# Who adds the second experts' sums: GpSimd's two passes or VectorE's, and the order of a round around them

## What is computed

```python
# end of the second layer's ffn: its two experts per token are summed, then normalized with a gain
fused = sum((topk_vals[:, :, i:i + 1] * outs[i] for i in range(TOP_K)))
return _layer_norm(residual + fused, ln_gamma, ln_beta)
...
# third layer, attention block (mLSTM), 4 heads of 64
D = jnp.exp(log_D - max_log_D)
C = qk * D
normalizer = jnp.maximum(jnp.abs(C.sum(-1, keepdims=True)), jnp.exp(-max_log_D))
h = jnp.einsum('bnst,bntd->bnsd', C / (normalizer + EPS_BACKEND), vh)
hn = (h - mean) * jax.lax.rsqrt(var + NORM_EPS) * outnorm_weight
...
# third layer, feed-forward block, with x_prev the token before
xr = mu_r * x + (1.0 - mu_r) * x_prev
xk = mu_k * x + (1.0 - mu_k) * x_prev
r = jax.nn.sigmoid(jnp.einsum('btc,dc->btd', xr, W_r))
k_act = jnp.square(jax.nn.relu(jnp.einsum('btc,dc->btd', xk, W_k)))
out = r * jnp.einsum('btc,dc->btd', k_act, W_v)
```

## Time and profile before

| | us |
|---|---|
| median of 3 runs | 1398.53 |
| lowest and highest run | 1395.99, 1401.62 |
| the profiled execution | 1400.19 |
| its span | 1398.1 |
| TensorE busy in it | 1258.8 (90%) |
| VectorE busy | 852.8 (61%) |
| ScalarE busy | 474.4 (34%) |
| GpSimd busy | 463.3 (33%) |

### The profile page before, as it was taken

How to read it: one execution, slowest core, us unless ns; L and a number is a source line. 1 busy time by engine, 2 the same in 40 slices (tenths; PEclk the granted TensorE clock), 3 DMA queues, 4 the chain that set the end, 5 groups by cost and what they waited for, 6 DMA issues and landing times. The chain is left out here.

```text
span 1398.1 us, 31670 instructions
## 1 busy us (share of the span) xinstructions
PE 1258.8 (90%) x9966; PEld 1008.9 (72%) x9966; DVE 852.8 (61%) x2809; ACT 474.4 (34%) x1119; POOL 463.3 (33%) x435
## 2 busy tenths in 40 slices
PE   5899799997899998899999888897899998899995
PEld 4677589995566665789887666686566665799995
DVE  5788544445577876444575476755567776465563
ACT  3555211112556554011111244453556654111110
POOL 1145612223134334423122256533134343222231
PEclk9999899999999999999999998999999999999998
DMA  9101234422111401464655100000001011646523
GB/s 312 66 17 36 93 103 139 136 65 80 34 36 40 164 33 51 140 205 149 198 174 168 28 8 1 1 1 24 8 17 48 32 40 53 207 100 150 145 46 87
DMA packets 87556, 120.07 MB, mean 86 GB/s; under 512 B 11248, under 2 KB 64752, under 8 KB 87152
## 3 DMA queue, kind: packets, MB, share of 16 engines
q1 hardware_dynamic: 48656, 55.20, 12.9%
q10 hardware_dynamic: 25632, 34.85, 7.6%
q0 software_dynamic: 13152, 28.54, 7.2%
HBM read 82.53 MB, written 38.13 MB: 86 GB/s over the span
## 5 line engine op out<-in xcount | busy, mean ns | idle before, releaser
L1349 PEld LDWEIGHTS bank<-f_xT,f_up 128*128 128x128 f32 x2144 | 253.6, 192 | 13.3 <-issue 6.3
L1349 PE MATMUL bank<-f_xT,f_up 128*128 128x128 f32 x2144 | 258.5, 276 | 2.4 <-DVE f_xT L1225 2.1
L415 DVE TENSOR_REDUCE mha_nmax<-bank 128x2 f32<-128x512 f32 x256 | 170.0, 686 | 117.2 <-PE bank L558 93.5
L1358 PE MATMUL bank<-f_down,f_hT 128*128 128x256 f32 x832 | 199.5, 382 | 4.4 <-DVE f_hT L1266 2.3
L308 ACT ACTIVATE l_took<-bank 128x512 f32<-128x512 f32 x256 | 139.0, 598 | 129.8 <-PE bank L566 129.8
L558 PE MATMUL bank<-l_took,mha_q 32*128 32x256 f32 x1024 | 146.3, 402 | 34.5 <-DVE mha_nmax L415 22.1
L1358 PEld LDWEIGHTS bank<-f_down,f_hT 128*128 128x128 f32 x832 | 149.4, 190 | 24.8 <-DVE f_hT L1266 4.6
L1114 POOL DMA_INDIRECT yout<-f_y,f_to x66 | 81.1, 1229 | 244.9 <-DVE f_y L1302 107.0
L558 PEld LDWEIGHTS bank<-l_took,mha_q 32*128 32x128 f32 x1024 | 90.1, 186 | 74.5 <-DVE mha_nmax L415 45.0
L566 PE MATMUL bank<-l_took 32*128 32x256 f32 x1024 | 142.8, 400 | 0.7 <-ACT l_took L308 0.7
L1165 ACT ACTIVATE f_hT<-bank,f_b 128x128 f32<-128x128 f32 x148 | 46.4, 364 | 276.0 <-PE bank L1349 276.0
(11 more groups left out here) (293 smaller groups left out, 2284.9 us busy)
## 6 DMA issues: line engine op xcount, KB each, us to landing
l_took<-rows SPq DMA_DIRECT2D x91, 132.0 KB
f_up<-in_W ACTq DMA_DIRECT2D x23, 512.0 KB, 4.8
f_down<-in_W ACTq DMA_DIRECT2D x18, 512.0 KB, 5.4
l_took<-rows SPq DMA_DIRECT2D x21, 264.0 KB
f_up<-in_W SPq DMA_DIRECT2D x9, 512.0 KB, 7.3
ring<-yout SPq DMA_DIRECT2D x8, 512.0 KB, 3.9
mha_ctxT<-in_ctxT SPq DMA_DIRECT2D x16, 256.0 KB, 2.9
f_down<-in_W SPq DMA_DIRECT2D x6, 512.0 KB, 7.5
```

What stands on the lines that cost most here:

```text
L415: vector.tensor_reduce(nmax[:, p, :, at], ps_s[n % 2][:, :].rearrange("p (k s) -> p k s", s=S), AX.X, ALU.min).then_inc(max_ready, 1)
L1349: ins = pe.matmul(into, up[q][i][:, c, m * P:(m + 1) * P], xT[:, c, :], start=c == 0, stop=c == DC - 1)
L1358: ins = pe.matmul(ps_y[:, 0:D], hT[:, m, :], down[q][:, m, :], start=m == 0, stop=m == HC - 1)
```

## The change

Six things, all in l2:

- GpSimd's z_add is gone, and VectorE's z_normalize. VectorE does z_centre and z_in for all batches: in rounds 0 to 4 z_centre stands where z_normalize stood, and z_in at the end of the round. GpSimd's z_root_of comes ahead of normalize instead of behind it.
- VectorE's f_normalize comes ahead of gate_rows.
- mean_and_var and z_mean_and_var come ahead of the weights of heads 2 and 3; they stood behind them, the latter behind the first mix.
- ScalarE's squares come ahead of squared_relu.
- On TensorE, the values of heads 0 and 1 come ahead of turn_f; a fill of 1 stands between the second spread and turn_z in rounds 1 to 7 (it stood in round 7 alone); round 0's fill of 1 becomes 2; turn_m comes ahead of turn_x.
- z_scaled and z_gained, two semaphores, are gone.

```diff
@@ gpsimd
-            def z_add(b):
-                pool.wait_ge(z_scaled, b + 1 - RING)
-                z_ = fused[:, b % RING, :, :]
-                pool.tensor_tensor(z_, z_, gamma[:, :].unsqueeze(1).to_broadcast([P, TPB, D]), ALU.mult).then_inc(z_gained, 1)
-                pool.wait_ge(z_gained, b + 1 - RING)
-                x = X[:, pair(b), :]
-                pool.tensor_tensor(x, x, z_, ALU.add).then_inc(z_added, 1)
...
+                if w_ + 3 < B:
+                    z_root_of(w_ + 3)
                 if w_ + 2 < B:
                     normalize(w_ + 2)
-                if w_ + 3 < B:
-                    z_root_of(w_ + 3)
-                    z_add(w_ + 3)
@@ scalar
-                if w_ >= LAG:
-                    squared_relu(w_ - LAG)
                 if now:
                     squares(w_)
                 if w_ >= LAG:
+                    squared_relu(w_ - LAG)
                     receptance(w_ - LAG)
@@ vector
-            def z_normalize(b):
...
@@ vector, the round
-                if more:
-                    gate_rows(w_ + 1)
                 if w_ >= LAG:
                     f_normalize(w_ - LAG)
                 if more:
+                    gate_rows(w_ + 1)
                     gates_in(w_ + 1)
+                if w_ + 2 < B:
+                    mean_and_var(w_ + 2)
+                if w_ + 3 < B:
+                    z_mean_and_var(w_ + 3)
                 if now:
                     weigh(w_, 2)
                     weigh(w_, 3)
-                if w_ + 2 < B:
-                    mean_and_var(w_ + 2)
                 if w_ >= LAG:
                     mix(w_ - LAG, 1, k_mixed)
-                if w_ + 3 < B:
-                    z_mean_and_var(w_ + 3)
...
                 if w_ + 3 < B:
-                    z_normalize(w_ + 3)
+                    z_centre(w_ + 3)
...
                 if w_ >= LAG:
                     outputs(w_ - LAG)
+                if w_ + 3 < B:
+                    z_in(w_ + 3)
@@ tensor
-                if w_ == B - 1:
+                if now and w_:
                     fill(w_, 1)
                 if more:
                     turn_z(w_ + 1)
                 if now:
                     qk(w_, 1)
+                    values(w_, 0)
+                    values(w_, 1)
...
-                if now:
-                    values(w_, 0)
-                    values(w_, 1)
                 if w_ == 0:
-                    fill(w_, 1)
+                    fill(w_, 2)
...
+                if more:
+                    turn_m(w_ + 1)
                 if w_ + 2 < B:
                     turn_x(w_ + 2)
-                if more:
-                    turn_m(w_ + 1)
```

More of the change, by code:

```diff
@@ L1869, in l2 @@
         fused_in, gamma_in = [sem(f"fused{r}_in") for r in range(RING)], sem("gamma_in")
-        z_ready, z_root, z_scaled, z_gained, z_added = sem("z_ready"), sem("z_root"), sem("z_scaled"), sem("z_gained"), sem("z_added")
+        z_ready, z_root, z_added = sem("z_ready"), sem("z_root"), sem("z_added")
         w, mu = sb("w", [P, 3, DC, D]), sb("mu", [P, 2, DC])
@@ L2114, in z_mean_and_var @@
                 moments_of(z_moments, z_stats, z_var, z_ready, b, fused[:, b % RING, :, :])
-            def z_normalize(b):
-                vector.wait_ge(z_root, b + 1)
-                for i in range(TPB):
-                    z_ = fused[:, b % RING, i, :]
-                    ins = vector.tensor_scalar(z_, z_, z_moments[:, b, i, 0:1], z_rstd[:, b, i:i + 1], ALU.subtract, ALU.mult)
-                ins.then_inc(z_scaled, 1)
             def z_centre(b):
@@ L2125, in z_centre @@
                 for i in range(TPB):
-                    z_ = fused[:, b, i, :]
+                    z_ = fused[:, b % RING, i, :]
                     ins = vector.scalar_tensor_tensor(out=z_, in0=z_, scalar=z_moments[:, b, i, 0:1], in1=gamma[:, :],
@@ L2134, in z_in @@
                     x = X[:, TPB * b + i, :]
-                    ins = vector.scalar_tensor_tensor(out=x, in0=fused[:, b, i, :], scalar=z_rstd[:, b, i:i + 1], in1=x,
+                    ins = vector.scalar_tensor_tensor(out=x, in0=fused[:, b % RING, i, :], scalar=z_rstd[:, b, i:i + 1], in1=x,
                                                       op0=ALU.mult, op1=ALU.add)
```

## The result

| | before | after |
|---|---|---|
| median, us | 1398.28 (6 runs) | 1392.73 (6 runs) |
| lowest and highest | 1395.99, 1401.62 | 1389.21, 1394.83 |
| span of the profiled execution | 1398.1 | 1391.8 |
| third layer, its begin to K8 | 195.7 | 190.3 |

What follows compares the result with a forecast made beforehand. The prediction took VectorE's line of work to bound the kernel. Its terms, -2.1 - 7.9 - 1.2 + 2.5 + 1.3 - 2.0 = -9.4 us, taken from the median 1398.53, gave 1389 us, range 1383 to 1399.

Steps and rivals of the forecast that it cites:

- Steps 1 and 3: Round from project_k: z_centre before gains hidden (0.88 us); TensorE, reaching turn_z after the gates' rows, holds the line by 1.
- The rival of small steps: Handovers in rounds 0 to 6 cost half a microsecond more each: +5 to 6 us, about 1394.5, chance 0.15.
- Step 2, the late relu: Squares before the relu delay TensorE's project_v, costing 0.7 us in rounds 1 to 6 with nothing to hide it.
- Step 4, z_in: Before f_mean_and_var, held beside GpSimd's passes over h: 0.2 to 0.6 us at worst, within slack, counted 0.
- Step 5 and the port: Copy of z to next project_k: 5.2 us. Rival: GpSimd's xn passes block the mixes, +6, 1395, chance 0.17.
- the rule that spoke against the forecast: Skill's rule: VectorE instructions with two SBUF inputs and GpSimd's SBUF reads fully block, holding mixes for a whole xn pass.
- Round 0: Round 0 and the way to round 1's project_k: VectorE earlier, partly held by turn_m and spread, -2.1 us.
- K1 to K4: Three rounds between project_k starts of rounds 1 and 4: 66.7 us becomes 3 x 19.6 = 58.8, -7.9.
- K4 to K5: Project_k of round 4 to that of round 5: 20.7 us becomes 19.5, the difference waiting for fT, -1.2.
- K5 to K6, K6 to K7: Project_k of rounds 5 to 7, no z batch left to save: 17.0 becomes 19.5 (+2.5), 16.2 becomes 17.5 (+1.3).
- K7 to the end: Tail from round 7's project_k: VectorE's 2.33 us wait for squares behind the relu goes, -2.0.
- a rival that decides for all rounds or none: TensorE's granted clock dips while its work is in the line: +3 us per round, 1404 to 1407, chance 0.11.

Runs made afterwards that it cites:

- the second measurement: The changed kernel run once more, unchanged, in a later job: 1397.01 us, ratio 0.9986.
- orders_only: The changed kernel with the z batch handed back to z_normalize and GpSimd's z_add, all new orders kept: 1396.07 us, ratio 0.9982.
- z_only: The kernel before with VectorE's z_centre and z_in for all batches, GpSimd's two passes gone, old orders kept: 1386.71 us, ratio 0.9890.
- fill_waits: The changed kernel with a dummy matmul in TensorE's waits before the last heads' values and before project_k: 1392.24 us, ratio 0.9944.
- turnf_first: The changed kernel with turn_f ahead of the first two heads' values again, in all rounds: 1394.61 us, ratio 0.9952.
- z_stats_fill: z_stats with a fill of one before the last heads' values and one before project_k, rounds 1 to 7: 1390.51 us, ratio 0.9945.
- z_stats: z_only with the statistics of X and the z batch ahead of the weights of heads 2 and 3: 1389.81 us, run again 1390.02.

## Why the prediction was right, and where its size was off

A gain was forecast and found, and 1392.73 lies within the range, 3.7 above the 1389 named. The size was off by more than the noise: 9.4 us lies outside the interval of 3.2 to 8.7. By the prediction's own chances this is not the likeliest case (more than 0.5% faster, 0.53) but the next one (within 0.5%, 0.40). That the median fell by just what the layer did, 5.6 and 5.4, is luck: in the second measurement it was 1.0 and 3.9. By its steps:

- *Steps 1 and 3, the line of a round:* right. Project_v at K + 5.12 (forecast 5.0), gates' rows at K + 13.6 (13.5), turn_z at K + 14.07 (14.1), copy of z to the next K 5.33 (5.2), the round 19.73 (19.6). That TensorE holds the line, by less than 1 us, fits orders_only too. The rival of small steps missed by the walk is out with it: 0.13 us a round, not 0.5.
- *Step 2, the late relu:* right in kind, 0.4 to 0.65 for 0.7.
- *Step 4, z_in:* it was held as told (2.25 for 0.88, f_mean_and_var 0.2 later), without moving K.
- *Step 5 and the port:* the mixes beside GpSimd's xn passes took 1.02, so that rival is out, and the rule that spoke against the forecast didn't hold: the mixes didn't stand for a whole pass. Here it was GpSimd that lost most: the two passes take 3.27, and 2.56 in z_only, where the first mix is nearly over when they begin.
- *Round 0:* -3.0 in one execution and -1.5 in the other, around the -2.1 forecast. The difference lies ahead of 790, where the clock differs between them. From the last qk before the loop (789.86 before, 789.23 and 788.86 after) to K1 it is 24.09 in both and 25.97 before: -1.9.
- *K1 to K4:* -5.8 for -7.9, and *K4 to K5:* +1.7 for -1.2. **These two terms failed, both by the clock:** the sum put nothing for dips in the new order, and two came, worth 4.5 us. Without dips (fill_waits) they are -7.5 and -1.1.
- *K5 to K6, K6 to K7:* +2.5 for +2.5, +1.4 for +1.3. turnf_first gave back 1.25 in each: turn_f behind the values is half of what was paid in the first and nearly all of it in the second.
- *K7 to the end:* -2.2 for -2.0. All of the wait for the squares went.

I had the dips as a rival that decides for all rounds or none, at 3 us each and against it the high share of TensorE's busy time. What I hadn't drawn from my own walk is that the new order puts two waits of 0.7 us right ahead of project_k. The statistics ahead of the last weights make the first of them; the second stood there before (0.84). Two dips came, worth 1.7 and 2.8, not five. The sign that the prediction set for this rival, a clock under 0.95 over rounds 1 to 4, did come, at 0.94, but it was a poor sign: over the same rounds the kernel before had 0.92. In the kernel before there is a dip between each K and the next from K1 to K4, and the prediction names only the one at 0.50 in the earlier trace rows. The windows K1 to K2 and K3 to K4 before, and TensorE ahead of the dip in K2 to K3:

```profile
815.80:837.70 21.90, 19.02 (x130) 14.11 (x128) 16.26 (x48) 9.22 (x20) 12.94 (x12) 0.92 0.05 13
860.60:882.50 21.90, 18.89 (x127) 14.20 (x127) 16.35 (x48) 9.22 (x20) 13.04 (x12) 0.92 0.01 2
...
842.81 0.20 PEld L2399 LDWEIGHTS bank<-consts,l_g 128*128 128x128 f32 x2 [1.14 <-DVE l_g L2201]
...
846.32 0.52 PEld L2405 LDWEIGHTS bank<-consts,l_m_rows 128*128 128x128 f32 x4 [1.15 <-DVE l_m_rows L2207]
```

It comes behind two waits too, 1.14 and 1.15, for gains and for the maxima; the same waits stand in the other z rounds. It made K2 to K3 22.96. The other two, of 3 to 4 us, left no mark (21.85 and 21.84, both at 0.92): VectorE held the line there, and TensorE's slow work ran beside it. So a dip costs only where TensorE is in the line, and by making TensorE the line the new order put a price on every dip. The forecast had taken the old ones as gone, and put none in their place.

A second miss is not one of size. I priced the change as a whole and never the z sums alone. The numbers were in the walk: I had written that nothing is left to save in rounds 5 and 6, and that three edits of order are paid there. A full-clock z round is 18.4 with the old order and 19.73 with the new one. From the layer's begin to K8, z_only is 17.1 us shorter than before and the changed kernel 5.4 (3.9 in the second execution): the orders give 11.7 us back, 7.5 of them without any dip (fill_waits less z_only), though the one in round 7 brings 2.3.

The Trainium skill ("TensorE: Matmul & The Clock Gate", Part 1: The HAM clock gate) says that TensorE's clock has two levels, by how busy the engine has been of late. The loads of project_k at 3.06 and 1.59 us agree with the two levels, and z_stats_fill with the cause.

What stays open: why, with the same two waits in each round, the changed kernel dips in rounds 1 and 4, orders_only in none, and z_stats in all four; and where the 4 us that the fills save in the layer go in the medians. Only the changed kernel and z_stats have two traces, the others one, and the rest of the program may simply hide them.

## What to carry to other kernels

When a change is a bundle, price each edit by itself before summing: here one edit was worth more than the bundle, since the reorders made TensorE the line and left the moved sums little to save. When work is put ahead of an instruction on which TensorE waits, count the idle time that this places in front of its next long block, for it can cost the clock as well as the wait, and a low clock is paid for only where TensorE is in the line. And where the rest of a program varies by more than the change brings, read the changed stretch by its own repeating marks.

## What was not expected of the hardware

- The clock's dips repeated in the same rounds in two executions: 21.42 and 21.41, 22.47 and 22.46 us after; 20.45 and 20.36, 20.46 and 20.42 in z_stats.
- A fill of one in each of two waits of 0.7 to 0.84 us took all of them away between K1 and K5 (0 of 8 rounds, for 18 of 28 without these fills), and where VectorE held TensorE up anyway it cost nothing in the round (19.73 both ways).
- Dips of 3 to 4 us in rounds that VectorE held cost nothing (21.85 and 21.84 us, with a clock of 0.92).
- VectorE and GpSimd gave way to each other differently by the kind of instruction. Beside GpSimd's whole-batch tensor_tensor, a VectorE pair with two SBUF inputs took 2.25 instead of 0.88. Beside its tensor_scalar passes the same kind of pair took 1.02, and it was GpSimd's pair that grew, 2.56 to 3.27.
